# One in nine: the second attention's channel blocks take nine thirds of a tile instead of eight, and its four groups lie 56 thirds apart instead of 54

## The reference, cut to what matters

```python
# layer 0
h = layernorm(x) * (1 + ca) + sa
x = x + ga * L0_attn(h)         # delta-rule recurrence with 64x64 states
h = layernorm(x) * (1 + cb) + sb
x = x + gb * L0_ffn(h)          # silu(gate) * up, 2048 hidden, ternary weights, rms norm
# layer 1
h = layernorm(x) * (1 + ca) + sa
x = x + ga * L1_attn(h)         # the "second attention"
h = layernorm(x) * (1 + cb) + sb
x = x + gb * L1_ffn(h)          # silu(gate) * up, 1408 hidden, integer codes

def L1_attn(hidden):            # per channel, over time
    xk, xv, xr = hidden * mix + shifted * (1 - mix)      # three mixes
    k, v, r = xk @ Wk.T, xv @ Wv.T, sigmoid(xr @ Wr.T)
    # running maximum, numerator and denominator of a decayed softmax over time
    rwkv = wkv_scan(time_decay, time_first, k, v)
    return (r * rwkv) @ Wo.T
```

## Time and profile before

| | us |
|---|---|
| median of three runs | 1276.56 |
| the profiled execution, its own time | 1278.01 |
| its span in the profile | 1275.9 |
| TensorE busy in the span | 1103.2 |
| VectorE busy | 870.8 |
| ScalarE busy | 529.6 |
| GpSimd busy | 169.4 |
| mean granted TensorE clock | 0.907 |

### The profile page before, as it was taken

The page is one execution under the profiler, slowest core; times in us unless marked ns, Lnnn a source line. Parts: engine busy times, 40 slices in busy tenths (PEclk is TensorE's granted clock), DMA queues, the critical chain, the costliest instruction groups (busy, mean ns, idle before and its releaser), DMA issues. The chain is left out here.

```text
span 1275.9 us, 13090 instructions
## 1 busy us (share of the span) xinstructions
PE 1103.2 (86%) x4385; PEld 550.7 (43%) x4432; DVE 870.8 (68%) x1602; ACT 529.6 (42%) x1101; POOL 169.4 (13%) x143
## 2 busy tenths in 40 slices
PE   5566777767998989988889889899997999989997
PEld 5434653444443344434344334344443444434443
DVE  3557765654666767987768887668886587874554
ACT  2433554415554347535236344154542253431321
POOL 3000000001111131113022121112202000100100
PEclk9667677657999899999899989999999999989999
DMA  7510111040322033313122002113010011100000
GB/s 223 180 34 33 34 50 34 17 165 22 111 84 83 1 113 94 110 55 109 60 77 67 17 25 66 34 34 112 25 58 8 1 58 34 42 33 1 1 33 33
DMA packets 47523, 75.55 MB, mean 59 GB/s; under 512 B 8320, under 2 KB 16000, under 8 KB 47328
## 3 DMA queue, kind: packets, MB, share of 16 engines
q1 hardware_dynamic: 47168, 74.62, 18.5%
q0 software_dynamic: 288, 0.09, 0.1%
HBM read 66.16 MB, written 8.54 MB: 59 GB/s over the span
## 5 line engine op out<-in xcount | busy, mean ns | idle before, releaser
L1590 PE MATMUL g_g<-h,wt 128*128 128x512 f16 x1728 | 399.3, 379 | 8.2 <-DVE hid L1872 2.4
L1590 PEld LDWEIGHTS g_g<-h,wt 128*128 128x128 bf16 (+1 forms) x1728 | 167.5, 98 | 225.0 <-issue 32.3
L1604 PE MATMUL g_d<-wt,parts 128*128 128x512 bf16 (+1 forms) x831 | 203.5, 385 | 10.5 <-DVE tmp L1702 3.5
L1513 PE MATMUL g_o<-shared 128*128 128x512 f32 x384 | 180.2, 612 | 16.7 <-ACT hf L2082 9.8
L2179 ACT ACTIVATE parts<-hid 128x512 f16<-128x512 f32 x108 | 68.0, 629 | 295.9 <-DVE hid L1872 290.4
L1865 DVE SCALAR_TENSOR_TENSOR hid<-th,g_g 128x512 f32<-128x512 f32 x108 | 73.5, 681 | 158.9 <-ACT th L2172 158.9
L1604 PEld LDWEIGHTS g_d<-wt,parts 128*128 128x128 f16 x864 | 83.9, 99 | 119.4 <-issue 21.1
L2289 POOL TENSOR_TENSOR acc<-acc,sqh 128x512 f32<-128x512 f32 x52 | 77.3, 1487 | 322.6 <-ACT sqh L2185 322.6
L1513 PEld LDWEIGHTS g_o<-shared 128*128 128x128 f32 x384 | 74.3, 196 | 98.9 <-issue 71.6
L1877 DVE TENSOR_TENSOR parts<-hid,parts 128x512 f16<-128x512 f32 x108 | 84.8, 785 | 31.8 <-ACT parts L2179 31.6
L1522 PE MATMUL g_o<-shared 128*128 128x512 f32 x128 | 64.2, 649 | 10.2 <-DVE shared L1949 5.2
(11 more groups left out here) (318 smaller groups left out, 1577.5 us busy)
## 6 DMA issues: line engine op xcount, KB each, us to landing
shared<-in_w SPq DMA_DIRECT2D x48, 256.0 KB, 2.7
x<-in_codes SPq DMA_DIRECT2D x32, 264.0 KB, 3.1
w_raw<-in_wt SPq DMA_DIRECT2D x16, 512.0 KB, 3.7
x<-in_wmod SPq DMA_DIRECT2D x7, 1024.0 KB, 5.2
wmod<-in_wmod SPq DMA_DIRECT2D x5, 1024.0 KB, 10.4
codes_f<-x SPq DMA_DIRECT2D x32, 132.0 KB, 1.7
gates<-in_x SPq DMA_DIRECT2D x4, 1024.0 KB, 5.8
x<-in_x SPq DMA_DIRECT2D x4, 1024.0 KB, 5.7
```

What stands on the lines that cost most here:

```text
L1513: mm = nc.tensor.matmul(dst[:], w1[:, n % 4, k], xmix[:, w, k], start=(k == 0), stop=(k == KD - 1))
L1590: mm = nc.tensor.matmul(pg[i][:], wide[:, k, o:o + P], h16[f % 2][:, s, k], start=(s == 0 and k == 0), stop=(s == 1 and k == KD - 1))
L1604: mm = nc.tensor.matmul(pd[j][:], parts16[:, t % 3, s, j * P:(j + 1) * P], wd[:, m, :], start=(m == 0 and s == 0), stop=(done and s == 1))
```

## The change

Two constants in `groups`:

```diff
-    ATT = [54 + 54 * i for i in range(NG)]
+    ATT = [54 + 56 * i for i in range(NG)]
...
-    PERIOD, FIRST = 8, 11
+    PERIOD, FIRST = 9, 11
```

## The result

The changed kernel takes 1257.26 us (median of four runs, 1255.15 to 1261.42) against 1276.85 us before (median of four): 0.985 of the time, 95% interval 0.9824 to 0.9876. The forecast was 1259.5 us with a range of 1250 to 1273. The profiled execution has a span of 1255.7 us, 20.2 less than before, and an own time of 1257.84 us.

What follows compares the result with a forecast made beforehand. TensorE, busy for 1103.2 of 1275.9 us, was taken to bound the kernel. Idle time (-7.9) and clock (-9) gave -17 us, a span of 1258.9, plus 0.7 rounded to 1259.5 us; range 1250 to 1273.

Steps and rivals of the forecast that it cites:

- What bounds it, and that the work stays: Whole kernel: TensorE bounds it and its work stays the same; only its idle time and lower-clock time can move.
- Idle time: TensorE's idle time in thirteen stretches of the four groups' attention: 45.8 us against 53.7, 7.9 us less.
- Group 0, middle: Tiles 25 to 32: only the first k waits for a bank, VectorE's lateness is mostly carried; idle 8.0 to 3.9 us.
- Group 0, end: Around tiles 33 and 34: residual and reciprocal halves delay the down, up and output products; idle 5.1 to 8.8 us.
- Group 3, start and end: Start: first `mixed` waits for its mix, 1.1 to 4.4 us idle; end: residual of tile 87 hides, 5.1 to 3.4.
- Clock: Loss from TensorE's lower clock in the low stretches: 10 instead of 18.7 us, 9 less; bounds nothing and 15.
- One for certain (tile 33): Group 0's end: the one low-clock stretch expected for certain after the change, 3.4 us; four others had even chance.
- The Trainium skill's rule on bank cycling: Low clock: the number of short gaps at PSUM bank changes counts; the clock's 9 us would be about 3.
- Rival A: Middle tile of each block: VectorE's load is not carried, TensorE loses 2.1 us a block; 1285 us, chance 0.08.
- Rival B: Gaps at tiles 33, 38, 43, 69, 77 start low stretches; clock doesn't recover; 1266 to 1273 us, chance 0.18.
- Rival C: Stalls only change places: group 0's end and starts of groups 1 and 3 absorb the middles' gain; 1276.5 us, chance 0.08.
- Rival D: Group 1's normalised rows and tile 33's residual hide: idle -17, clock -13, 1247 us, chance 0.06.

## Why the prediction was right

**What bounds it, and that the work stays.** Right. TensorE's work did not change, and but for 0.8 us in the head the difference is in its idle and low-clock time between 470 and 1182 us. After tile 93 the kernels are equal to 0.1 us of excess.

**The number is in part luck.** The two terms together were forecast at -17 us and came to -23.3. The total is only 3.2 us beside the forecast span because I had added them without taking off the idle time inside low stretches (1.8 us) and because the head came out 0.8 longer. And within the idle time, group 0's middle was 5.2 us too low and other places were too high.

**Idle time: -7.9 forecast, -13.1 measured.** The places of group 1 and group 2 came out within 1.8 us each. Three places did not, and they are the terms that were mis-sized:

- *Group 0, middle, 3.9 forecast, 9.1 measured.* The step that failed: "Only the first k waits, for a1's bank: 0.73 + 0.68 less the 0.86 of a2, 0.6 us." I priced the up product as if VectorE reached it at once. Ahead of it stand the first output (2.06 us) and a half reciprocal (1.74 us). The wait is 3.0 us; with the reciprocal moved it is 1.4. The same omission hid the wait of 3.2 us in tile 30: there ScalarE's high part waits for the up product, and the transposes' `hf` stands behind it. This fell to 1.85 when the reciprocal was moved.
- *Group 0, end, 8.8 forecast, 5.3 measured.* The terms that were too large are the down product's wait for the residual's banks, "some 5.3 us", measured 2.7 (0.8 and 1.9), the up half's, 1.7 against 1.1, and the first output product's, 1.8 against 1.4. I had carried VectorE's lateness into the residual from a middle without waits. That the waits of tiles 27 to 30 let VectorE catch up would explain it but isn't shown: with the reciprocal moved, tiles 25 to 32 idle 2.9 us less, and tiles 33 to 35 idle 4.95 us, not more than the 5.28 of the changed kernel. Middle and end together were forecast at 12.7 us and measured at 14.4.
- *Group 3, start and end, 7.8 forecast, 2.4 measured.* The first `mixed` of tile 77 waits for its mix as I said, but 1.2 us, not 3.1. At the end I had 3.4 us stick out in tiles 88 to 90; the trace has 0.6 in tiles 86 to 92.

**Clock: -9 forecast, -10.2 measured.** Right in the sum. "One for certain (tile 33)" was wrong: tile 33 has 3.8 us of idle time in three waits (0.8, 1.9, 1.1) and no low stretch; those of tiles 27, 30, 43 and 69 came.

**The Trainium skill's rule on bank cycling** (Trainium skill, TensorE: Matmul & The Clock Gate, "A second HAM failure mode: psum-queue depth-cycling") would have had the clock's part near 3 us. The measured 10.2 speaks for the size of the waits rather than their number. So does tile 27, where a bank wait fell from 3.0 to 1.4 us, with the same bank changes, and the low stretch behind it went. But size alone doesn't decide it either, as the last section shows.

**Rival A** (VectorE's load isn't carried) is out. Group 3's blocks, tiles 78 to 85 of the changed kernel, keep TensorE busy for 67.67 of 69.56 us. The trace agrees that VectorE works in order: the up product of tile 27 has its matmuls by 549.72 us and starts at 552.49, when the reciprocal is done. But what this costs here depends on which product stands behind the long operation. **Rival B** is out by the clock's 10.2 us. (Its upper end was wrong in itself: 8 to 11 us less than 1276.6 is 1266 to 1269, not 1273.) **Rival C** has a true core: with a distance of 54 the starts get better by 8.6 us of excess, and tiles 42 to 54 worse by 4.4. **Rival D** named two places, and both came out better than the forecast; its idle time of -17 and clock of -13 were not reached.

## What to carry to other kernels

When two lists of work are interleaved with a period, count where each long operation lands for every repeat: a period that is a multiple of the host's step puts a long operation always in the same slot, for good or bad, and then it can pay to move that one operation. Here an operation of 1.74 us, moved by one third in the blocks of two groups, was worth 12 us, some 8.5 of them where the order was changed. Price a wait for a bank through the whole in-order queue of the engine that frees it. And give TensorE's longest waits a second price for the clock: in tiles 27 and 30 it was as large as the idle time that was taken away. It is a price on average and not for every execution, as the next section shows.

## What the runs showed of the hardware that I had not expected

The same wait of TensorE is followed by a low stretch in one kernel and by none in another. At the start of tile 69 the changed kernel waits 3.16 us, the kernel with group 1 moved 3.15 us, at nearly the same time. Windows from 950 to 970 us, the changed kernel, then the other:

```profile
950.00:970.00 20.00, 16.84 (x66) 8.32 (x64) 12.70 (x16) 11.73 (x19) 4.46 (x3) 0.83 0.06 16
```

```profile
950.00:970.00 20.00, 16.85 (x79) 8.47 (x78) 15.32 (x20) 13.10 (x21) 6.07 (x4) 1.00 0.05 19
```

PEclk 0.83 of 20 us is 3.4 us lost, and TensorE does 13 matmuls fewer in the window at the same busy time. The other three kernels with this wait unchanged and within 8 us of it (group 0 as before, one reciprocal later, both later) show 1.00 too; the repeat of the changed kernel shows 0.83. In tile 19 it is plainer. All kernels but the one with all groups in the last third have the same order up to there, and all of them wait 2.69 us for normalised rows. Four of these eleven profiled executions have a low stretch of 1.7 us at that wait (nine thirds alone, group 1 moved, both halves later, group 2 at 164), seven have none. The changed kernel, then the one with group 1 moved, each with its wait and its window:

```profile
481.39 0.63 PE L1412 MATMUL g_o<-ident,xn 128*128 128x128 f32 x4 [2.69 <-DVE xn L1662]
478.00:492.00 14.00, 11.26 (x60) 5.92 (x59) 10.32 (x22) 9.37 (x17) 3.80 (x3) 1.00 0.30 88
```

```profile
476.75 0.66 PE L1412 MATMUL g_o<-ident,xn 128*128 128x128 f32 x2 [2.69 <-DVE xn L1662]
473.36:487.36 14.00, 11.31 (x55) 6.05 (x53) 9.70 (x21) 8.76 (x16) 3.04 (x3) 0.88 0.31 88
```

So part of the clock's loss belongs to the execution and not to the kernel, and what makes the difference stays open. It means that 2 to 4 us between two of these kernels can be the clock's and not the order's. The start of tile 17, ahead of which nothing differs, also lies between 460.7 and 467.3 us in the twelve profiled executions. Between the runs of one kernel there are up to 10 us; how much of that is the head's, the profiled executions alone can't say.
